# Top-32 attention: the third eight is sunk by GpSimd, the fourth eight found a tile later, and half of the marking done by ScalarE

## The chip, the cores and the metric

The kernel runs on one core of one Trainium2 chip. The metric is the device time of one execution in microseconds (us). TensorE (PE) multiplies, VectorE (DVE), ScalarE (ACT) and GpSimd (POOL) work elementwise, SyncE (SP) issues transfers.

## The reference

Per batch of 8, with 512 queries, 1024 keys and 16 heads of 16 channels: of each row of scores only the 32 largest enter the softmax. An output projection, a gated residual and a mixture of experts follow.

```python
q = (query @ Wq.T + bq).reshape(Bn, Sq, H, DK).transpose(0, 2, 1, 3)
k = (key @ Wk.T + bk).reshape(Bn, -1, H, DK).transpose(0, 2, 1, 3)
scores = jnp.einsum('bhqd,bhkd->bhqk', q, k) / np.sqrt(DK)
vals, idx = jax.lax.top_k(scores, 32)
p = jax.nn.softmax(vals, axis=-1)
ctx = jnp.einsum('bhqk,bhqkd->bhqd', p, gathered_v)
x = x + jnp.tanh(g_xattn[0]) * (ctx @ Wo.T + bo)
x = x + jnp.tanh(g_ffn[0]) * mixture_of_experts(layernorm(x))
```

## The kernel before

The program runs in stages, each a function with one program per engine: project (queries, keys and values, queries and keys cut into three bf16 parts), attend, repair, route, experts, combine. The change lies in attend, with two lines in repair.

attend works on 512 tiles T of 128 queries and one head, four tiles (QT) to a head H, sixteen (TILES) to an iteration I. Every engine's program is written out by hand as a loop over steps s; what it does in a step is for tiles some steps back, and semaphores alone tie the engines together.

- TensorE: `scores` (L415) makes the scores of a tile in ps_s, two steps ahead. `mark` (L429, L436) makes the transposed scores of a whole head for two of its eight key blocks in ps_e (L429, with three rows of the row's maximum to subtract), and adds -2^100 through `big` for each score that `side` marks as under the 32nd (L436). `count` (L446) sums the marks, `turn_peak`, `values` and `turn_out` handle the maxima, the product with the values and the turned result.
- ScalarE: `copy` (L505) brings ps_s to one of four buffers `sc`, once the tile four back has been marked (`sided`); `shift` (L510) takes the maxima; `exp` (L516) takes ps_e to pT; `take_out` (L523) the result; `count_mask` and `sum_counts` once in sixteen tiles.
- VectorE: `chunks` (L564) finds the best eight of each of 24 chunks of a tile. The step is cut into eight slots of three chunks; behind each slot stands one instruction for the tile before: `pick` (first eight), `best_of_rest`, `cull`, `pick` (second eight), `cull`, `round_of` (third eight, L598), `cull` (L591, the third eight taken out of 80 candidates), `round_of` (fourth eight). The last of the fourth eight is the 32nd value. `invert` and `normalise` come once a head.
- GpSimd: `to_sides` (L664) writes 1 into `side` where a score is under the 32nd value, 0 elsewhere; `cut_peaks` cuts a head's maxima into bf16 parts; `find_odd` tells, once in sixteen tiles, whether the chunks may have held back a candidate.

repair sums what count and find_odd have left and makes a list of the tiles whose marks are not exactly 32 a row. It then does each of these again from the start, one after the other (a memset of g_s, L795, on GpSimd opens each).

```python
    FIRST = 7
    SIDES = 12
    END = NT + 12
```

FIRST is by how many steps the first mark of a head trails its first tile.

Of the kernel before, what the change touches and what calls it, by code (L numbers as in the profile page):

```python
# [7 lines left out]
BF16 = mybir.dt.bfloat16  # L8
# [285 lines left out]
def attend(nc, pl, io, scr, keep):  # L294
# [5 lines left out]


    G, TILES, KB, HG, DK, VW, KR, S, S2, QT = pl.G, pl.TILES, pl.KB, pl.HG, pl.DK, pl.VW, pl.KR, pl.S, pl.S2, pl.QT
    CH, NA, NC = pl.CH, pl.NA, pl.NC
    NT, NH = pl.ITER * TILES, pl.ITER * HG
    SHIFT = 3
    PAIRS = KB // 2
    FIRST = 7
    SIDES = 12
    END = NT + 12
    assert pl.TT == pl.ITER and QT == 4 and PAIRS == QT and KB == 8  # L310
    with ExitStack() as ctx:
# [8 lines left out]
        identb = sb("a_identb", [P, P], BF16)  # L320
        big = sb("a_big", [P, P], BF16)
        stack = sb("a_stack", [P, VW])
        sc = sb("a_sc", [P, 4, S2])
# [4 lines left out]
        above = sb("a_above", [P, 2, TILES, 2])  # L328
        rest = sb("a_rest", [P, 2, QT])
        peak = sb("a_peak", [P, 2, QT, SHIFT], BF16)  # L330
# [26 lines left out]
        culled = sem("a_culled")  # L357
        topped = sem("a_topped")
        odd_part = sem("a_odd_part")
# [4 lines left out]
        shifted = sem("a_shifted")  # L364
        sided = sem("a_sided")
        marked = sem("a_marked")
# [37 lines left out]
        def _(pe):  # L404
            pe.wait_ge(consts, 8 + TILES)

# [12 lines left out]
            def mark(H, n):  # L419

                u, j = H // HG % 2, H % HG
                if n == 0:
                    pe.wait_ge(shifted, H + 1)
                if H or n:
                    pe.wait_ge(expd, PAIRS * H + n)
                for i in range(2):
                    k = 2 * n + i
                    keys = slice(k * P, (k + 1) * P)
                    nc.tensor.matmul(ps_e[:, i * S:(i + 1) * S], ks[:, u, j, keys], qs[:, u, j, :], start=True, stop=False)  # L429
                if n == 0:  # L430
                    pe.wait_ge(sided, QT * H + QT)
                for i in range(2):
                    k = 2 * n + i
                    keys = slice(k * P, (k + 1) * P)
                    for qt in range(QT):
                        mm = nc.tensor.matmul(ps_e[:, i * S + qt * P:i * S + (qt + 1) * P],  # L436
                                              side[:, (QT * H + qt) % SIDES, keys], big[:], start=False, stop=qt == QT - 1)
                mm.then_inc(marked, 1)

            def count(T):  # L440
                I, i = T // TILES, T % TILES
                if i == 0 and I:
                    pe.wait_ge(summed, I)
                pe.wait_ge(sided, T + 1)
# [35 lines left out]

            for s in range(-2, END):
                H, n = head_at(s, FIRST)
                if H is not None:
                    mark(H, n)
                if 0 <= s - 4 < NT:
                    count(s - 4)
# [3 lines left out]
                H, n = head_at(s, 5)  # L490
                if H is not None and n == 0:
                    turn_peak(H)
                H, n = head_at(s, 13)
                if H is not None and n == 0:
                    turn_out(H)
                if s + 2 < NT:
                    scores(s + 2)

        @block.scalar
        def _(act):  # L500
            def copy(T):
                act.wait_ge(scored, T + 1)
                if T >= 4:
                    act.wait_ge(sided, T - 3)
                nc.scalar.copy(sc[:, T % 4, :], ps_s[:]).then_inc(copied, 1)  # L505

# [30 lines left out]

            for s in range(-1, END):
                if s + 1 < NT:
                    copy(s + 1)  # L540
                H, n = head_at(s, 6)
                if H is not None and n == 0:
                    shift(H)
                H, n = head_at(s, FIRST)
                if H is not None:
                    exp(H, n)
                H, n = head_at(s, 12)
                if H is not None and n == 0:
                    take_out(H)
                I, i = divmod(s - 4, TILES)  # L550
                if i == TILES - 1 and 0 <= I < pl.ITER:
                    sum_counts(I)
                I, i = divmod(s, TILES)
                if i == 9 and I < pl.ITER:
                    count_mask(I)

        @block.vector
        def _(dve):
            SLOTS = 8

            def chunks(T, n0, n1):
                c = cand[:, T % 4, :]
                for n in range(n0, n1):
                    ins = nc.vector.max(c[:, 8 + n:8 + n + 7 * CH + 1:CH], sc[:, T % 4, pl.cut[n]:pl.cut[n + 1]])  # L564
                if n1 == CH:
                    ins.then_inc(chunked, 1)

            def pick(T, r):
# [4 lines left out]
                else:  # L573
                    dve.wait_ge(culled, 3 * T + 1)
                nc.vector.max(top[:, T // TILES % 2, T % TILES, 8 * r:8 * r + 8], cand[:, T % 4, 8:8 + (r + 1) * CH]
# [6 lines left out]
            def cull(T, r):  # L582

                m = top[:, T // TILES % 2, T % TILES, 8 * r:8 * r + 8]
                if r < 2:
                    dve.wait_ge(picked, 2 * T + r + 1)
                    c = cand[:, T % 4, 8:8 + (r + 1) * CH]
                else:
                    dve.wait_ge(topped, 2 * T + 1)
                    c = cand[:, T % 4, 0:8 + NA]  # L590
                nc.vector.match_replace(c, m, c, TAKEN).then_inc(culled, 1)  # L591

            def round_of(T, r):

                if r == 2:
                    dve.wait_ge(rested, T + 1)
                dve.wait_ge(culled, 3 * T + r)
                nc.vector.max(top[:, T // TILES % 2, T % TILES, 8 * r:8 * r + 8], cand[:, T % 4, 0:8 + NA]).then_inc(topped, 1)  # L598

# [13 lines left out]
            for s in range(END):  # L613
                if s < NT:
                    dve.wait_ge(copied, s + 1)
                H, n = head_at(s, 14)
                for p in range(SLOTS):
# [7 lines left out]
                    if 0 <= T < NT:  # L625
# [6 lines left out]
                        elif p == 3:  # L632
                            pick(T, 1)
                        elif p % 2 == 0:
                            cull(T, p // 2 - 1)
                        else:
                            round_of(T, (p - 1) // 2)

        @block.gpsimd
        def _(pool):  # L640
            nc.gpsimd.memset(ks[KR:KR + SHIFT], -1.0).then_inc(consts, 1)
            pool.wait_ge(consts, 1)
            nc.gpsimd.memset(ident[:], 0.0).then_inc(set0, 1)
            nc.gpsimd.memset(row_of[:], 0.0).then_inc(set0, 1)
# [5 lines left out]
            for c in range(P // VW):  # L650
                nc.gpsimd.affine_select(out=stack[:], in_=stack[:], compare_op=ALU.not_equal, fill=1.0, base=-VW * c,
                                        pattern=[[-1, VW]], channel_multiplier=1).then_inc(consts, 1)
                pool.wait_ge(consts, 3 + c)
            nc.gpsimd.tensor_scalar(big[:], ident[:], -FLOOR, None, ALU.mult).then_inc(consts, 1)
# [4 lines left out]
            def to_sides(T):  # L659

                pool.wait_ge(topped, 2 * T + 2)
                if T >= SIDES:
                    pool.wait_ge(marked, PAIRS * ((T - SIDES) // QT + 1))
                nc.gpsimd.tensor_scalar(side[:, T % SIDES, :], sc[:, T % 4, :],  # L664
                                        top[:, T // TILES % 2, T % TILES, pl.TOPK - 1:pl.TOPK], None, ALU.is_lt
                                        ).then_inc(sided, 1)

# [28 lines left out]

            for s in range(2, NT + 2):
                to_sides(s - 2)
                H, n = head_at(s, 4)
                if H is not None and n == 0:  # L700
                    cut_peaks(H)
                if (s - 2) % TILES == TILES - 1:
                    find_odd((s - 2) // TILES)


def repair(nc, pl, io, scr, keep):
# [7 lines left out]
    with ExitStack() as ctx:  # L714
# [146 lines left out]
        def _(dve):  # L861
# [3 lines left out]
            def link(ins):  # L865
# [7 lines left out]
            dve.wait_ge(in_flat, 16)  # L873
            link(V.tensor_scalar(bad[:].rearrange("p (i n) -> p n i", n=TILES), flat[:], float(P * (S2 - pl.TOPK)), None,
                                 ALU.not_equal))
            link(V.scalar_tensor_tensor(out=bad[:], in0=ps_t[0][0:1, 0:NT], scalar=0.0, in1=bad[:], op0=ALU.is_gt,
# [805 lines left out]
```

## Time and profile before

| | us |
|---|---|
| median of 3 runs (lowest, highest) | 3369.7 (3368.29, 3371.82) |
| the profiled execution | 3371.16 |
| its span, first to last instruction | 3369.4 |
| VectorE busy in the span | 2730.0 |
| TensorE busy | 2526.4 |
| GpSimd busy | 1863.3 |
| ScalarE busy | 1440.1 |
| first to last start of a chunk search | 246.5 to 2168.6 |

The span runs from the first to the last instruction of the profiled execution, and the busy times are inside it. Averages over the span mix stages: attention holds some 1922 us of it, and repair, routing, experts and combination follow. Matmuls are pipelined and their ends modelled, so that a busy TensorE is not one at its peak.

### The profile page before, as it was taken

The page shows a single profiled execution, that of the slowest core. Times are in us where ns is not written, and L with a number is a line of the kernel's source. Part 1 is how long each engine was busy: PE and PEld are TensorE (multiplying, and loading weights), DVE is VectorE, ACT ScalarE, POOL GpSimd, SP SyncE. Part 2 cuts the span into 40 slices and gives each one's busy share as a digit, 9 for nine tenths or more (in the row PEclk, how much of TensorE's full clock was granted, in tenths as well). Part 3 has the DMA queues.
Part 4 walks back from the last instruction along what each step waited for, and adds up shares of the span by engine and source line. Part 5 has one row for each costly group of instructions (what it writes and reads, how often), then busy time and mean ns, then how long its engine had stood idle before and what let it go on. Part 6 is the DMA issues. An engine that isn't in the chain of part 4 may idle for free. (4 is left out here: it accounts for less than half of the span.)

```text
span 3369.4 us, 64915 instructions
## 1 busy us (share of the span) xinstructions
PE 2526.4 (75%) x17711; PEld 1590.3 (47%) x17712; DVE 2730.0 (81%) x20227; ACT 1440.1 (43%) x1942; POOL 1863.3 (55%) x1381
## 2 busy tenths in 40 slices
PE   7827788777778787877787877724705999999990
PEld 5413333333333333333333333313605999999990
DVE  6739999999999999999999999754705666666753
ACT  2215666666666666666666666501101222222220
POOL 1018888888888888888888888600172111111107
PEclk9868999999999999999999999955757999999995
DMA  6870212111121111212112111011222111122106
GB/s 200 249 183 25 53 32 62 32 44 50 32 62 32 47 47 32 62 32 47 47 32 62 32 46 48 1 40 42 76 95 101 65 60 61 49 69 70 67 30 192
DMA packets 141931, 219.60 MB, mean 65 GB/s; under 512 B 22433, under 2 KB 103585, under 8 KB 138497
## 3 DMA queue, kind: packets, MB, share of 16 engines
q1 hardware_dynamic: 116608, 171.43, 18.5%
q0 software_dynamic: 9472, 29.37, 2.8%
q10 hardware_dynamic: 15488, 14.68, 1.3%
q8 instruction: 140, 2.29, 0.3%
q14 instruction: 223, 1.82, 0.2%
HBM read 142.02 MB, written 73.40 MB: 64 GB/s over the span
## 5 line engine op out<-in xcount | busy, mean ns | idle before, releaser
L564 DVE MAX8 a_cand<-a_sc 128x8 f32<-128x43 f32 (+1 forms) x12288 | 1723.7, 215 | 49.8 <-ACT a_sc L505 49.7
L664 POOL TENSOR_SCALAR a_side<-a_sc,a_top 128x1024 bf16<-128x1024 f32 x512 | 1455.0, 2842 | 334.9 <-DVE a_top L598 329.9
L505 ACT COPY a_sc<-a_ps_s 128x1024 f32<-128x1024 f32 x512 | 518.2, 1012 | 780.6 <-POOL a_side L664 720.1
L516 ACT ACTIVATE a_pT<-a_ps_e 128x1024 f32<-128x1024 f32 x512 | 526.5, 1028 | 13.4 <-PE a_ps_e L436 9.7
L415 PE MATMUL a_ps_s<-a_ks,a_qs 96*128 96x512 bf16 x1024 | 320.1, 395 | 246.7 <-ACT a_sc L505 193.6
L429 PE MATMUL a_ps_e<-a_qs,a_ks 99*128 99x512 bf16 x1024 | 316.1, 391 | 179.6 <-ACT a_pT L516 179.0
L468 PE MATMUL a_ps_o<-a_pT,a_vs 128*32 128x512 f32 x2048 | 428.0, 692 | 1.1 <-ACT a_pT L516 1.1
L1351 POOL TENSOR_TENSOR e_wl<-e_raw,e_wh 128x2048 fp32r<-128x2048 f32 x24 | 110.5, 4603 | 521.7 <-DVE e_wh L1488 521.7
L1391 PE MATMUL e_ps_gu<-e_xh,e_wl 128*128 128x256 f32 x1280 | 364.2, 285 | 5.9 <-DVE e_xl L1471 4.0
L1393 PE MATMUL e_ps_gu<-e_xh,e_wh 128*128 128x256 f32 x1280 | 363.4, 284 | 0.0
L1392 PE MATMUL e_ps_gu<-e_xl,e_wh 128*128 128x256 f32 x1280 | 363.4, 284 | 0.0
L436 PEld LDWEIGHTS a_ps_e<-a_big,a_side 128*128 128x128 bf16 x4096 | 284.6, 100 | 128.8 <-issue 12.4
L446 PE MATMUL a_ps_c<-a_side,a_row_of 128*16 128x512 bf16 x1024 | 331.0, 407 | 0.0
L591 DVE MATCH_REPLACE8 a_cand<-a_top,a_cand 128x24 f32<-128x24 f32 (+2 forms) x1536 | 331.0, 215 | 0.0
L436 PE MATMUL a_ps_e<-a_big,a_side 128*128 128x128 bf16 x4096 | 328.9, 225 | 0.0
L415 PEld LDWEIGHTS a_ps_s<-a_ks,a_qs 96*128 96x128 bf16 x1024 | 71.6, 109 | 516.8 <-ACT a_sc L505 341.7
L1503 DVE SCALAR_TENSOR_TENSOR e_sg<-e_th,e_ps_gu 128x256 f32<-128x256 f32 x320 | 134.3, 420 | 192.7 <-ACT e_th L1451 177.3
L1451 ACT ACTIVATE e_th<-e_ps_gu 128x256 f32<-128x256 f32 x320 | 122.6, 383 | 340.0 <-PE e_ps_gu L1393 329.5
L429 PEld LDWEIGHTS a_ps_e<-a_qs,a_ks 99*128 99x128 bf16 x1024 | 76.5, 98 | 379.3 <-issue 211.1
L598 DVE MAX8 a_top<-a_cand 128x8 f32<-128x80 f32 x1024 | 252.2, 246 | 2.0
L1391 PEld LDWEIGHTS e_ps_gu<-e_xh,e_wl 128*128 128x128 f32 x1280 | 247.1, 193 | 7.2 <-DVE e_xl L1471 4.7
L1392 PEld LDWEIGHTS e_ps_gu<-e_xl,e_wh 128*128 128x128 f32 x1280 | 247.2, 193 | 0.0
(206 smaller groups left out, 4120.4 us busy)
## 6 DMA issues: line engine op xcount, KB each, us to landing
scr_v<-p_vp SPq DMA_DIRECT2D x32, 512.0 KB, 5.9
a_vs<-scr_v SPq DMA_DIRECT2D x32, 512.0 KB, 5.8
a_mask<-in_mask SPq DMA_DIRECT2D x32, 512.0 KB, 6.6
scr_k<-p_kp SPq DMA_DIRECT2D x96, 128.0 KB, 2.4
a_ks<-scr_k SPq DMA_DIRECT2D x32, 384.0 KB, 4.5
a_qs<-scr_q SPq DMA_DIRECT2D x192, 64.0 KB, 5.2
scr_disp<-a_zeros SPq DMA_DIRECT2D x32, 320.0 KB, 7.0
e_xin<-scr_disp SPq DMA_DIRECT2D x40, 256.0 KB, 2.7
```

The source lines that it names most:

```text
L415: mm = nc.tensor.matmul(ps_s[:, h * 512:(h + 1) * 512], qs[0:KR, u, j, qt * P:(qt + 1) * P], ks[0:KR, u, j, h * 512:(h + 1) * 512], start= ...
L429: nc.tensor.matmul(ps_e[:, i * S:(i + 1) * S], ks[:, u, j, keys], qs[:, u, j, :], start=True, stop=False)
L436: mm = nc.tensor.matmul(ps_e[:, i * S + qt * P:i * S + (qt + 1) * P], side[:, (QT * H + qt) % SIDES, keys], big[:], start=False, stop=qt = ...
L446: mm = nc.tensor.matmul(ps_c[0:TILES, :], row_of[:, i, :], side[:, T % SIDES, h * 512:(h + 1) * 512], start=(i == 0 and h == 0), stop=(i = ...
L468: mm = nc.tensor.matmul(ps_o[VW * c:VW * (c + 1), :], vs[:, u, k, VW * j:VW * (j + 1)], pT[:, k, :], start=(half == 0), stop=(half == 1), ...
L505: nc.scalar.copy(sc[:, T % 4, :], ps_s[:]).then_inc(copied, 1)
L516: nc.scalar.activation(pT[:, 2 * n:2 * n + 2, :].rearrange("p k q -> p (k q)"), ps_e[:], ACT.Exp).then_inc(expd, 1)
L564: ins = nc.vector.max(c[:, 8 + n:8 + n + 7 * CH + 1:CH], sc[:, T % 4, pl.cut[n]:pl.cut[n + 1]])
L664: nc.gpsimd.tensor_scalar(side[:, T % SIDES, :], sc[:, T % 4, :], top[:, T // TILES % 2, T % TILES, pl.TOPK - 1:pl.TOPK], None, ALU.is_lt) ...
L1391: nc.tensor.matmul(out, al, bh, start=(k == 0), stop=False)
L1392: nc.tensor.matmul(out, ah, bl, start=False, stop=False)
L1393: mm = nc.tensor.matmul(out, ah, bh, start=False, stop=(k == n - 1))
```

## The change

The third cull leaves VectorE. After the third eight, GpSimd does `sink`: it makes `gone`, which is -3e38 wherever a candidate is at or above the 24th value, and adds it to the candidates as `left`. `round_of(T, 3)` takes the fourth eight from `left`, one step later than before. `to_sides` stays on GpSimd for the first two tiles of a head. For the other two GpSimd does `step_under`, two operations on one column that give `next_under`, the next number under the 32nd value, and ScalarE marks by Sign of next_under minus score: -1 for a kept score, 1 for one under it. So `mark` first adds -2^100 to these two tiles through `onesb` and `floor`, then the sides, and the scores last. There are six buffers `sc` for four; marks, counts and what follows them come one step later.

```diff
-    FIRST = 7
+    FIRST = 8
+    SCORES = 6
+    HALF = QT // 2
     SIDES = 12
-    END = NT + 12
+    END = NT + 14
...
+        def sided_by(T):
+
+            by = T % QT // HALF
+            return sided[by], T // QT * HALF + T % HALF + 1
...
+                if n == 0:
+                    for by in sided:
+                        pe.wait_ge(by, HALF * H + HALF)
                 for i in range(2):
                     k = 2 * n + i
                     keys = slice(k * P, (k + 1) * P)
-                    nc.tensor.matmul(ps_e[:, i * S:(i + 1) * S], ks[:, u, j, keys], qs[:, u, j, :], start=True, stop=False)
-                if n == 0:
-                    pe.wait_ge(sided, QT * H + QT)
-                for i in range(2):
-                    k = 2 * n + i
-                    keys = slice(k * P, (k + 1) * P)
+                    nc.tensor.matmul(ps_e[:, i * S + HALF * P:(i + 1) * S], onesb[:], floor[:], start=True, stop=False)
                     for qt in range(QT):
-                        mm = nc.tensor.matmul(ps_e[:, i * S + qt * P:i * S + (qt + 1) * P],
-                                              side[:, (QT * H + qt) % SIDES, keys], big[:], start=False, stop=qt == QT - 1)
+                        nc.tensor.matmul(ps_e[:, i * S + qt * P:i * S + (qt + 1) * P], side[:, (QT * H + qt) % SIDES, keys],
+                                         big[:], start=False, stop=False)
+                    mm = nc.tensor.matmul(ps_e[:, i * S:(i + 1) * S], ks[:, u, j, keys], qs[:, u, j, :],
+                                          start=False, stop=True)
                 mm.then_inc(marked, 1)
...
         @block.scalar
         def _(act):
+            def to_sides(T):
+
+                act.wait_ge(under_set, T // QT * HALF + T % HALF + 1)
+                if T >= SIDES:
+                    act.wait_ge(marked, PAIRS * ((T - SIDES) // QT + 1))
+                nc.scalar.activation(side[:, T % SIDES, :], sc[:, T % SCORES, :], ACT.Sign, bias=next_under[:, T % 8:T % 8 + 1],
+                                     scale=-1.0).then_inc(sided[1], 1)
+
             def copy(T):
                 act.wait_ge(scored, T + 1)
-                if T >= 4:
-                    act.wait_ge(sided, T - 3)
-                nc.scalar.copy(sc[:, T % 4, :], ps_s[:]).then_inc(copied, 1)
+                if T >= SCORES:
+                    act.wait_ge(*sided_by(T - SCORES))
+                nc.scalar.copy(sc[:, T % SCORES, :], ps_s[:]).then_inc(copied, 1)
...
                 if s + 1 < NT:
                     copy(s + 1)
-                H, n = head_at(s, 6)
+                if 0 <= s - 4 < NT and (s - 4) % QT >= HALF:
+                    to_sides(s - 4)
+                H, n = head_at(s, 7)
...
+                else:
+                    dve.wait_ge(sunk, T + 1)
+                    src = left[:, T % 2, :]
+                nc.vector.max(top[:, T // TILES % 2, T % TILES, 8 * r:8 * r + 8], src).then_inc(topped[r - 2], 1)
...
-                        elif p % 2 == 0:
+                        elif p == 2 or p == 4:
                             cull(T, p // 2 - 1)
-                        else:
-                            round_of(T, (p - 1) // 2)
+                        elif p == 5:
+                            round_of(T, 2)
+                    if p == 6 and 0 <= s - 2 < NT:
+                        round_of(s - 2, 3)
...
+            def step_under(T):
+
+                n = T // QT * HALF + T % HALF + 1
+                pool.wait_ge(topped[1], T + 1)
+                last = top[:, T // TILES % 2, T % TILES, pl.TOPK - 1:pl.TOPK]
+                one = slice(T % 8, T % 8 + 1)
+                nc.gpsimd.tensor_scalar(gap[:, one], last, 1.0 + 2.0 ** -23, -2.0 ** -124, ALU.mult, ALU.add
+                                        ).then_inc(gap_set, 1)
+                pool.wait_ge(gap_set, n)
+                nc.gpsimd.tensor_scalar(next_under[:, one], last, 1.0 - 2.0 ** -24, gap[:, one], ALU.mult, ALU.min
+                                        ).then_inc(under_set, 1)
+
+            def sink(T):
+
+                src, g = cand[:, T % 4, 0:8 + NA], gone[:, T % 2, :]
+                pool.wait_ge(topped[0], T + 1)
+                nc.gpsimd.tensor_scalar(g, src, top[:, T // TILES % 2, T % TILES, 23:24], TAKEN, ALU.is_ge, ALU.mult
+                                        ).then_inc(found, 1)
+                pool.wait_ge(found, T + 1)
+                nc.gpsimd.tensor_tensor(left[:, T % 2, :], src, g, ALU.add).then_inc(sunk, 1)
...
-            for s in range(2, NT + 2):
-                to_sides(s - 2)
+            for s in range(2, NT + 3):
+                if s - 2 < NT:
+                    sink(s - 2)
+                T = s - 3
+                if T >= 0 and T % QT < HALF:
+                    to_sides(T)
+                elif T >= 0:
+                    step_under(T)
```

In repair the expected sum of marks is P x (1024 - 32) for the first two tiles of a head, as before for all, and P x (1024 - 64) for the other two.

On VectorE, in the middle of attention, from one tile's second cull to the next tile's first instruction (a_top holds the eights, a_cand the candidates). Before:

```order
L591 MATCH_REPLACE a_cand<-a_top,a_cand 128x48 [waits a_picked]
L564 MAX a_cand<-a_sc 128x8 x3
L598 MAX a_top<-a_cand 128x8 [waits a_culled,a_rested]
L564 MAX a_cand<-a_sc 128x8 x3
L591 MATCH_REPLACE a_cand<-a_top,a_cand 128x80 [waits a_topped]
L564 MAX a_cand<-a_sc 128x8 x3
L598 MAX a_top<-a_cand 128x8 [waits a_culled]
L564 MAX a_cand<-a_sc 128x8 [waits a_copied]
L564 MAX a_cand<-a_sc 128x8 x2
L575 MAX a_top<-a_cand 128x8 [waits a_chunked]
```

Now:

```order
L592 MAX a_cand<-a_sc 128x8 x3
L626 MAX a_top<-a_cand 128x8 [waits a_culled,a_rested]
L592 MAX a_cand<-a_sc 128x8 x3
L626 MAX a_top<-a_left 128x8 [waits a_sunk]
L592 MAX a_cand<-a_sc 128x8 x3
L592 MAX a_cand<-a_sc 128x8 [waits a_copied]
L592 MAX a_cand<-a_sc 128x8 x2
L603 MAX a_top<-a_cand 128x8 [waits a_chunked]
```

The cull over 80 candidates is gone, the round that reads a_left, of the tile before, has its slot, and two slots of three searches follow each other.

On GpSimd, in the second half of a head's cycle, now (before, each tile had one L664 there):

```order
L716 TENSOR_SCALAR a_gone<-a_cand,a_top 128x80 [waits a_topped2]
L719 TENSOR_TENSOR a_left<-a_cand,a_gone 128x80 [waits a_found]
L696 TENSOR_SCALAR a_side<-a_sc,a_top 128x1024 [waits a_marked,a_topped3]
L716 TENSOR_SCALAR a_gone<-a_cand,a_top 128x80 [waits a_topped2]
L719 TENSOR_TENSOR a_left<-a_cand,a_gone 128x80 [waits a_found]
L696 TENSOR_SCALAR a_side<-a_sc,a_top 128x1024 [waits a_marked,a_topped3]
L742 CAST a_peak<-a_top 128x4 [waits a_picked,a_peak_turned]
```

A sink stands before each marking, and the head's cut_peaks (its first row is the last one here) behind the second of two markings.

## Rows read from the trace of the kernel before

**Rows 1.** The page, part 1: busy us (share of the span) x instructions.

```profile
PE 2526.4 (75%) x17711; PEld 1590.3 (47%) x17712; DVE 2730.0 (81%) x20227; ACT 1440.1 (43%) x1942; POOL 1863.3 (55%) x1381
```

**Rows 2.** Busy time by stretch: PE, PEld, DVE, ACT, POOL, PEclk, DMA share, GB/s.

```profile
1200.00:1600.00 400.00, 318.13 (x2246) 143.77 (x2243) 399.60 (x3781) 247.72 (x293) 326.19 (x237) 0.95 0.18 43
...
460.00:520.00 60.00, 49.78 (x339) 22.32 (x339) 60.00 (x570) 37.31 (x45) 49.04 (x36) 0.91 0.15 39
```

**Rows 3.** The page, part 5, VectorE's chunk searches: busy, mean ns, idle before.

```profile
L564 DVE MAX8 a_cand<-a_sc 128x8 f32<-128x43 f32 (+1 forms) x12288 | 1723.7, 215 | 49.8 <-ACT a_sc L505 49.7
```

**Rows 4.** Timeline of VectorE within one step: start us, us, what.

```profile
1201.39 0.44 DVE L564 MAX8 a_cand<-a_sc 128x8 f32<-128x42 f32 x3
...
1203.72 0.44 DVE L564 MAX8 a_cand<-a_sc 128x8 f32<-128x42 f32 x3
1204.03 0.11 DVE L591 MATCH_VALUE_LOAD a_cand<-a_top,a_cand 128x8 f32 x1
...
1204.23 0.45 DVE L564 MAX8 a_cand<-a_sc 128x8 f32<-128x42 f32 x3
...
1204.69 0.44 DVE L564 MAX8 a_cand<-a_sc 128x8 f32<-128x42 f32 x3
...
1205.09 0.44 DVE L564 MAX8 a_cand<-a_sc 128x8 f32<-128x42 f32 x3
```

**Rows 5.** Timeline of the second step, in brackets idle time before.

```profile
249.39 0.40 DVE L564 MAX8 a_cand<-a_sc 128x8 f32<-128x42 f32 x3
...
252.88 2.86 POOL L664 TENSOR_SCALAR a_side<-a_sc,a_top 128x1024 bf16<-128x1024 f32 x1 [15.66 <-DVE a_top L598]
...
253.08 0.41 DVE L564 MAX8 a_cand<-a_sc 128x8 f32<-128x42 f32 x3
```

**Rows 6.** Groups of GpSimd: busy us, mean ns, idle before.

```profile
L664 POOL TENSOR_SCALAR a_side<-a_sc,a_top 128x1024 bf16<-128x1024 f32 x512 | 1455.0, 2842 | 334.9 <-DVE a_top L598 329.9 <-PE a_ps_e L436 4.2 <-issue 0.2
...
L695 POOL TENSOR_TENSOR a_peak<-a_rest,a_peak 128x4 bf16<-128x4 f32 x128 | 26.3, 206 | 10.2
...
L672 POOL TENSOR_TENSOR a_above<-a_top 128x32 f32<-128x32 f32 x32 | 9.4, 295 | 0.0
L675 POOL TENSOR_SCALAR a_above<-a_above 128x32 f32<-128x32 f32 x32 | 9.3, 292 | 3.0
...
L654 POOL TENSOR_SCALAR a_big<-a_ident 128x128 bf16<-128x128 f32 x1 | 0.6, 566 | 0.1
```

**Rows 7.** Groups of ScalarE.

```profile
L516 ACT ACTIVATE a_pT<-a_ps_e 128x1024 f32<-128x1024 f32 x512 | 526.5, 1028 | 13.4 <-PE a_ps_e L436 9.7
L505 ACT COPY a_sc<-a_ps_s 128x1024 f32<-128x1024 f32 x512 | 518.2, 1012 | 780.6 <-POOL a_side L664 720.1 <-PE a_ps_s L415 60.5
...
L853 ACT ACTIVATE g_ex<-g_s,g_nmax 128x1024 f32<-128x1024 f32 x5 | 5.7, 1148 | 69.2 <-DVE g_nmax L910 69.2
```

**Rows 8.** Timeline of TensorE, turns, scores and a mark.

```profile
1208.77 0.39 PE L456 MATMUL a_ps_r<-a_identb,a_peak 128*3 128x128 bf16 x4 [0.20 <-POOL a_peak L695]
...
1210.00 0.60 PE L415 MATMUL a_ps_s<-a_ks,a_qs 96*128 96x512 bf16 x2
1210.43 0.60 PE L429 MATMUL a_ps_e<-a_qs,a_ks 99*128 99x512 bf16 x2
1210.87 0.61 PE L436 MATMUL a_ps_e<-a_big,a_side 128*128 128x128 bf16 x8
1211.41 0.60 PE L446 MATMUL a_ps_c<-a_side,a_row_of 128*16 128x512 bf16 x2
```

**Rows 9.** First and last chunk search (view of line 564), and the stage's end.

```profile
L564 DVE MAX8 a_cand<-a_sc x12288: 183/214/261, 246.5 to 2168.6; 128x8 f32<-128x43 f32 x132, 128x8 f32<-128x42 f32 x67
...
2177.49 1.02 ACT L516 ACTIVATE a_pT<-a_ps_e 128x1024 f32<-128x1024 f32 x1 [1.22 <-PE a_ps_e L436]
...
2189.61 0.62 SPq L802 DMA_DIRECT2D g_flat<-lows  x1
```

**Rows 10.** Timeline of GpSimd in the repair stage.

```profile
2223.37 0.95 POOL L795 MEMSET g_s<- 128x1024 f32 x1 [20.52 <-DVEq L781]
...
2295.97 0.95 POOL L795 MEMSET g_s<- 128x1024 f32 x1 [23.17 <-DVEq L781]
```

More of the change, by code:

```diff
@@ L321, in attend @@
         big = sb("a_big", [P, P], BF16)
+        onesb = sb("a_onesb", [P, P], BF16)
+        floor = sb("a_floor", [P, HALF * P], BF16)
         stack = sb("a_stack", [P, VW])
-        sc = sb("a_sc", [P, 4, S2])
+        sc = sb("a_sc", [P, SCORES, S2])
         side = sb("a_side", [P, SIDES, S2], BF16)
@@ L328, in attend @@
         above = sb("a_above", [P, 2, TILES, 2])
+        gone = sb("a_gone", [P, 2, 8 + NA])
+        left = sb("a_left", [P, 2, 8 + NA])
+        gap = sb("a_gap", [P, 8])
+        next_under = sb("a_next_under", [P, 8])
         rest = sb("a_rest", [P, 2, QT])
@@ L357, in attend @@
         culled = sem("a_culled")
-        topped = sem("a_topped")
+        topped = [sem(f"a_topped{n}") for n in (2, 3)]
+        found = sem("a_found")
+        sunk = sem("a_sunk")
+        gap_set = sem("a_gap_set")
+        under_set = sem("a_under_set")
         odd_part = sem("a_odd_part")
@@ L364, in attend @@
         shifted = sem("a_shifted")
-        sided = sem("a_sided")
+        sided = [sem(f"a_sided_{n}") for n in ("pool", "act")]
         marked = sem("a_marked")
@@ L404, in _ @@
         def _(pe):
-            pe.wait_ge(consts, 8 + TILES)
+            pe.wait_ge(consts, 10 + TILES)
             def scores(T):
@@ L484, in _ @@
                     mark(H, n)
-                if 0 <= s - 4 < NT:
-                    count(s - 4)
+                if 0 <= s - 5 < NT:
+                    count(s - 5)
                 H, n = head_at(s, FIRST + 2)
@@ L489, in _ @@
                     values(H, n // 2)
-                H, n = head_at(s, 5)
+                H, n = head_at(s, 6)
                 if H is not None and n == 0:
                     turn_peak(H)
-                H, n = head_at(s, 13)
+                H, n = head_at(s, 14)
                 if H is not None and n == 0:
@@ L546, in _ @@
                     exp(H, n)
[L547 removed]
+                H, n = head_at(s, 13)
                 if H is not None and n == 0:
                     take_out(H)
[L550 removed]
+                I, i = divmod(s - 5, TILES)
                 if i == TILES - 1 and 0 <= I < pl.ITER:
@@ L642, in _ @@
             pool.wait_ge(consts, 1)
+            nc.gpsimd.memset(onesb[:], 1.0).then_inc(consts, 1)
+            nc.gpsimd.memset(floor[:], -FLOOR / P).then_inc(consts, 1)
             nc.gpsimd.memset(ident[:], 0.0).then_inc(set0, 1)
@@ L701, in _ @@
                     cut_peaks(H)
-                if (s - 2) % TILES == TILES - 1:
-                    find_odd((s - 2) // TILES)
+                if T >= 0 and T % TILES == TILES - 1:
+                    find_odd(T // TILES)
 def repair(nc, pl, io, scr, keep):
@@ L873, in _ @@
             dve.wait_ge(in_flat, 16)
-            link(V.tensor_scalar(bad[:].rearrange("p (i n) -> p n i", n=TILES), flat[:], float(P * (S2 - pl.TOPK)), None,
-                                 ALU.not_equal))
+            of_tile = bad[:].rearrange("p (i j t) -> p j t i", j=HG, t=QT)
+            sums = flat[:].rearrange("p (j t) i -> p j t i", t=QT)
+            half = QT // 2
+            for h, right in ((slice(0, half), P * (S2 - pl.TOPK)), (slice(half, QT), P * (S2 - 2 * pl.TOPK))):
+                ins = V.tensor_scalar(of_tile[:, :, h], sums[:, :, h], float(right), None, ALU.not_equal)
+            link(ins)
             link(V.scalar_tensor_tensor(out=bad[:], in0=ps_t[0][0:1, 0:NT], scalar=0.0, in1=bad[:], op0=ALU.is_gt,
```

28 lines of the change are left out of this document (12 added, 16 removed).

## The prediction

> **What bounds the kernel now.** I read the page first: VectorE is busy for 2730.0 of 3369.4 us, more than any other engine [rows 1]. Then the stretches: in the attention stage VectorE is busy for 399.6 of 400 us, TensorE for 318.1, GpSimd for 326.2 and ScalarE for 247.7 [rows 2]. Then the groups: over 12288 chunk searches VectorE stood 49.8 us before them, 49.7 of it once, before the first [rows 3]. So VectorE sets the pace of attention, and only what leaves its queue can shorten a tile. The last view is its order in time. A tile's step is 24 chunk searches in eight slots of three, with one instruction of the tile before behind each three. Three searches alone take 0.31 us (1203.72 to 1204.03), the slot with the third cull 0.51 (to 1204.23), the slot with a round 0.46 (to 1204.69), a whole step 3.70 (1201.39 to 1205.09) [rows 4]. One step in four also carries a reciprocal and a product, so the mean is 3.75: the searches start from 246.5 to 2168.6 us, 1922 us for 512 tiles [rows 9].
>
> **VectorE.** The third cull goes, two instructions by the row (value load and replace). Slots six and seven took 0.51 + 0.46; they become a slot with the fourth round, 0.46, and a bare slot, 0.31. That is 0.20 us a tile, on the path, and 512 x 0.20 = **102 us**. The new step is 3.55 on the mean, 14.2 us a head of four tiles.
>
> **GpSimd.** It gains two operations over 128x80 a tile (sink) and loses half of its 2.84 us markings. No row has 128x80. The nearest are 0.29 us for 128x32 (L672, L675) and 0.57 for 128x128 (L654) [rows 6]; I take 0.43 each, in the middle of the two, and 0.09 for each start behind a wait, 1.05 a sink, with 0.75 and 1.3 as ends. The two 128x1 steps for a tile that ScalarE marks I take at 0.27 each with their wait, by the 0.21 of the 128x4 rows (L695); cut_peaks has four such, 1.1. A head then costs 4 x 1.05 + 2 x 2.90 + 2 x 0.54 + 1.1 + 0.3 (find_odd, once in four heads) = 12.5 of 14.2 us, and 13.5 at the upper end. It stays hidden. The fourth round of a tile now waits for its sink, with all later VectorE work behind it. Tightest is the head's fourth tile, whose sink stands behind two markings and cut_peaks. From the second tile's sink, ready 2.85 us into a step: 1.05 + 2.90 + 1.05 + 2.90 + 1.1 + 1.05 = 10.05, done at 12.9, against 3 x 3.55 + 3.0 = 13.7 for the round's slot. That leaves 0.8 us, and none at the upper end. I cost it at nothing.
>
> **ScalarE.** Two Signs of 128x1024 a head, with a bias per partition. The row of the same form is the 1.15 us Exp of the repair stage (L853), against 1.03 for Exp without such a bias (L516) [rows 7]. A tile is then 1.01 + 1.03 + 1.15/2 + about 0.4 for the shorter copies and sums = 3.0 of 3.55 us. The Sign waits for next_under, which GpSimd sets early in the third step after the tile's own; behind the Sign stand an Exp and the next copy. That copy is needed more than a step later, since there are six score buffers where there were four. Nothing reaches VectorE.
>
> **TensorE.** Each mark gains two 256-column products with the ones, and the 512-column products move behind the sides. Two products of 512 columns take 0.44 us (1210.43 to 1210.87) [rows 8], so two of 256 take half of that, 0.22 a tile, and a mark goes from 0.98 (1210.43 to 1211.41) to 1.20; weight loads beside a busy array could hold it to the same or stretch it by their own, 0.1 each, to 1.4. At 318.1/400 x 3.75 = 2.98 us of busy time a tile, TensorE comes to 3.2 of 3.55.
>
> **The ends.** Two more fills at the start lie ahead of the loads: 0.3 us. At the end, the last search starts at 2168.6 and the next stage's first transfer at 2189.6, 21 us [rows 9]. The last head now waits for sink, a later round, next_under and two Signs, so that its first Exp (2177.49 now) comes some 2 us later behind the last search, and its marks are 0.22 longer each; 3 us with the start.
>
> **The repair.** A tile whose candidates may be wrong is flagged and done again, one after the other: five memsets of g_s, from 2223.37 to 2295.97 three tiles, 24.2 us each [rows 10]. The change alters who is flagged. Sink takes out everything at or above the 24th value, so that a tie of the 24th and 25th now flags the tile; Sign gives 0 for a score that equals next_under, one last bit under the 32nd, and flags it in two tiles of four. I counted both on the reference's inputs, with scores from the kernel's split into three bf16 parts and last bits disturbed 18 times: the old rule flags 3 to 6 tiles (the trace: 5), the new one 0 to 3 more, one or two in 14 of 18, and one in all three countings that gave 5 before. I take one, **+24 us**, and keep 0 (nothing) and 3 (73) as ends.
>
> **Sum.** The profiled execution took 3371.2 us, a span of 3369.4 and 1.8 around it; 3371.2 - 102 + 3 + 24 = 3296. The runs' median is 1.5 below that execution, so 3295.
>
> **A rule against this change.** VectorE's steps are as long beside GpSimd as without: the step from 249.39 to 253.08 takes 3.69 with GpSimd standing until 252.88 [rows 5], and 3.70 beside its markings [rows 4]. The Trainium skill (Perfetto Trace Analysis, Optimizing Scalar/DVE Operations) warns that the two share a read port, so that handing work from one to the other may not help; by that rule the sum would lose its gain, by the rows it keeps it.
>
> **Rivals.**
> 1. TensorE and ScalarE pace each other: the next mark waits for an Exp, each copy for its scores, and one step of a head has count, values and the turns on TensorE, then scores, copy, Sign and shift before the next Exp. Followed with no overlap across steps, a head's steps take about 3.0, 3.0, 5.5 and 2.4 us (the turns, 1208.77 to 1210.00, are 1.2 of it; a mark and an Exp 2.4) and 0.4 for mask and sums: 14.3 against 14.2. For it: stretches at the lower clock, granted 0.91 in one of 60 us [rows 2], which lengthen the TensorE part of 14.3 to some 14.8. Against it: the next mark can run beside copy and Sign, and six buffers smooth single slow heads. It would give 3295 + 13 to 3295 + 77, so 3308 to 3372. Chance 0.13.
> 2. Slower: GpSimd paces. It decides when a sink costs over 1.7 us, where a head reaches 15.0 us, today's 4 x 3.75. At 0.9 us an operation, which is more than twice what I interpolate, a head is 8.3 + 4 x 2.0 = 16.3, a tile 4.07, and 512 x (4.07 - 3.75) = +164, with ends and repair 3560. For it: two of the three new forms are in no row. Against it: 128x128 took 0.57. Chance 0.06.
> 3. Not what it says: the Sign does not resolve the last bit, and all 256 of its tiles are repaired, 256 x 24.2 = 6195 us more, 9490. For it: no row shows a Sign of such differences. Against it: the sign of a difference of neighbouring values needs no more than an exact subtraction. Chance 0.03. The Trainium skill (ScalarE: Activation LUTs, Step-by-step: what each stage is for) says that scale and bias are one fused step with a single rounding; by that, this does not happen. No run here shows it.
> 4. VectorE stands while GpSimd reads, the rule above as a mechanism: each sink would hold it for 0.86 us, 512 x (0.86 - 0.20) = +338, with ends and repair 3735. Rows 4 and 5 speak against. Chance 0.02.
>
> **How the numbers follow.** VectorE pacing has 0.76: with no further repair 3271 (0.17), one 3295 (0.33), two 3319 (0.18), three or more from 3343 (0.08). The range from 3267 to 3345 holds these but a little, and half of rival 1; outside are rivals 2 to 4 and the rest, 0.2. A measurement here tells 0.2%, 7 us. Faster by more: 0.75 and nearly all of rival 1, 0.86; within it 0.03; slower 0.11.
>
> **What would show it.** Right: a bare slot of 0.31 us and a step of 3.50 on VectorE; no idle time before the round on a_left; GpSimd's 128x80 operations near 0.43; Signs near 1.15 us; six memsets of g_s. Idle time of VectorE before its chunk searches, released by ScalarE's copies, would mean rival 1; before the round on a_left, rival 2. A span off by steps of 24 us with the step as forecast means that the flagged tiles were miscounted.

## The result, and the profile after

The changed kernel takes 3286.8 us in the median (3284.0 to 3290.2), and the kernel before 3369.0 in the same session (3367.5 to 3371.8): a ratio of 0.976, with a 95% interval of 0.974 to 0.977. The forecast was 3295, in a range from 3267 to 3345. The profiled execution took 3286.27 us with a span of 3284.6, so 84.8 of span are to be found.

The page, part 1, of the changed kernel: busy us (share of the span) x instructions, beside [rows 1].

```profile
PE 2541.3 (77%) x18762; PEld 1653.7 (50%) x18763; DVE 2632.4 (80%) x19222; ACT 1713.0 (52%) x2201; POOL 1735.8 (53%) x2664
```

The same stretch of attention as in [rows 2], with the columns of that view:

```profile
1200.00:1600.00 400.00, 337.92 (x2606) 165.80 (x2604) 399.68 (x3781) 321.22 (x366) 317.07 (x532) 0.99 0.19 46
```

VectorE is still busy for 399.7 of 400 us, so it still sets the pace. It passes the stage sooner because its step holds less. The view of its chunk searches (first and last start), as in [rows 9]:

```profile
L592 DVE MAX8 a_cand<-a_sc x12288: 179/195/238, 248.3 to 2060.9; 128x8 f32<-128x43 f32 x132, 128x8 f32<-128x42 f32 x67
```

The searches now take 2060.9 - 248.3 = 1812.6 us, 3.540 a tile; before, 1922.1 and 3.754. Its timeline within one step, to be laid beside [rows 4]:

```profile
1200.35 0.39 DVE L592 MAX8 a_cand<-a_sc 128x8 f32<-128x42 f32 x3
...
1202.53 0.21 DVE L626 MAX8 a_top<-a_cand 128x8 f32<-128x80 f32 x1
1202.68 0.39 DVE L592 MAX8 a_cand<-a_sc 128x8 f32<-128x42 f32 x3
1202.99 0.22 DVE L626 MAX8 a_top<-a_left 128x8 f32<-128x80 f32 x1
1203.13 0.70 DVE L592 MAX8 a_cand<-a_sc 128x8 f32<-128x42 f32 x6
1203.76 0.16 DVE L603 MAX8 a_top<-a_cand 128x8 f32<-128x24 f32 x1
1203.84 0.39 DVE L592 MAX8 a_cand<-a_sc 128x8 f32<-128x42 f32 x3
```

The step is 1200.35 to 1203.84, 3.49 us where it was 3.70. The two slots at issue are the one with the fourth round (1202.68 to 1203.13, 0.45) and the bare one, half of the six searches from 1203.13 to 1203.76 (0.31): 0.76 where they took 0.51 + 0.46.

What the other engines took over, from the groups of instructions (busy, mean ns of one, idle before):

```profile
L531 ACT COPY a_sc<-a_ps_s 128x1024 f32<-128x1024 f32 x512 | 516.8, 1009 | 166.5 <-PE a_ps_s L433 159.2
...
L524 ACT ACTIVATE a_side<-a_sc,a_next_under 128x1024 bf16<-128x1024 f32 x256 | 295.1, 1153 | 162.6 <-POOL a_next_under L709 162.6
...
L716 POOL TENSOR_SCALAR a_gone<-a_cand,a_top 128x80 f32<-128x80 f32 x512 | 293.9, 574 | 260.7 <-DVE a_top L626 260.5
L719 POOL TENSOR_TENSOR a_left<-a_cand,a_gone 128x80 f32<-128x80 f32 x512 | 180.6, 353 | 42.7
...
L626 DVE MAX8 a_top<-a_left 128x8 f32<-128x80 f32 x512 | 117.3, 229 | 3.7 <-POOL a_left L719 3.7
```

The last row of the groups is the one to look at: VectorE waited for GpSimd's sink for 3.7 us in all, and those stand at the end of the stage, once. ScalarE's copies no longer wait for GpSimd's marks (720 us in [rows 7]) but for TensorE's scores, 159 us, none of which reaches VectorE: its searches stood for a copy once, for 47.2 us before the first. From the start of a sink to the start of the marking behind it GpSimd takes 0.98 us:

```profile
1210.16 0.56 POOL L716 TENSOR_SCALAR a_gone<-a_cand,a_top 128x80 f32<-128x80 f32 x1
1210.81 0.35 POOL L719 TENSOR_TENSOR a_left<-a_cand,a_gone 128x80 f32<-128x80 f32 x1
1211.14 2.85 POOL L696 TENSOR_SCALAR a_side<-a_sc,a_top 128x1024 bf16<-128x1024 f32 x1
```

The price lies in the repair stage, in the timeline of GpSimd there, as in [rows 10]:

```profile
2098.17 0.95 POOL L854 MEMSET g_s<- 128x1024 f32 x1 [10.99 <-remote]
2119.51 0.95 POOL L854 MEMSET g_s<- 128x1024 f32 x1 [20.39 <-DVEq L840]
...
2215.25 0.95 POOL L854 MEMSET g_s<- 128x1024 f32 x1 [22.95 <-DVEq L840]
2250.03 0.20 POOL L1103 MEMSET r_ident<- 128x128 f32 x1 [33.83 <-POOLq L773]
```

In the kernel before, the first memset and r_ident's are these:

```profile
2201.89 0.95 POOL L795 MEMSET g_s<- 128x1024 f32 x1 [11.07 <-remote]
...
2331.12 0.20 POOL L1040 MEMSET r_ident<- 128x128 f32 x1 [34.20 <-POOLq L714]
```

There are six memsets where there were five, and from the first to r_ident's, which opens the next stage, it is 151.9 us; before, it was 129.2. The whole account of the span: searches -109.5, their start +1.8, from the last search to the repair stage's first transfer +4.1 (25.1 for 21.0), repair +22.6, all later stages -3.7; the sum is -84.7.

### The profile page after: what moved, and what is told of

The parts are those of the page before. It is cut to its first block and busy times, and to the rows that moved or that the text cites. A ratio compares the mean times of both kernels' runs of the same rounds, so it can differ in the third digit from the quotient of the medians.

```text
span 3284.6 us, 67760 instructions
## 1 busy us (share of the span) xinstructions
PE 2541.3 (77%) x18762; PEld 1653.7 (50%) x18763; DVE 2632.4 (80%) x19222; ACT 1713.0 (52%) x2201; POOL 1735.8 (53%) x2664
## 5 line engine op out<-in xcount | busy, mean ns | idle before, releaser
L592 DVE MAX8 a_cand<-a_sc 128x8 f32<-128x43 f32 (+1 forms) x12288 | 1614.1, 198 | 47.3 <-ACT a_sc L531 47.2
L696 POOL TENSOR_SCALAR a_side<-a_sc,a_top 128x1024 bf16<-128x1024 f32 x256 | 729.3, 2849 | 0.0
L450 PE MATMUL a_ps_e<-a_floor,a_onesb 128*128 128x256 bf16 x1024 | 285.1, 278 | 275.7 <-issue 136.3
L716 POOL TENSOR_SCALAR a_gone<-a_cand,a_top 128x80 f32<-128x80 f32 x512 | 293.9, 574 | 260.7 <-DVE a_top L626 260.5
L452 PE MATMUL a_ps_e<-a_big,a_side 128*128 128x128 bf16 x4096 | 400.9, 221 | 0.0
L454 PE MATMUL a_ps_e<-a_qs,a_ks 99*128 99x512 bf16 x1024 | 397.5, 388 | 0.0
L524 ACT ACTIVATE a_side<-a_sc,a_next_under 128x1024 bf16<-128x1024 f32 x256 | 295.1, 1153 | 162.6 <-POOL a_next_under L709 162.6
L486 PE MATMUL a_ps_o<-a_pT,a_vs 128*32 128x512 f32 x2048 | 372.8, 608 | 1.1 <-ACT a_pT L542 1.1
L452 PEld LDWEIGHTS a_ps_e<-a_big,a_side 128*128 128x128 bf16 x4096 | 318.2, 98 | 93.5 <-issue 2.3
L450 PEld LDWEIGHTS a_ps_e<-a_floor,a_onesb 128*128 128x128 bf16 x1024 | 100.6, 98 | 482.2 <-ACT a_pT L542 252.9
```

Of the source, the lines that this page charges most:

```text
L450: nc.tensor.matmul(ps_e[:, i * S + HALF * P:(i + 1) * S], onesb[:], floor[:], start=True, stop=False)
L454: mm = nc.tensor.matmul(ps_e[:, i * S:(i + 1) * S], ks[:, u, j, keys], qs[:, u, j, :], start=False, stop=True)
L486: mm = nc.tensor.matmul(ps_o[VW * c:VW * (c + 1), :], vs[:, u, k, VW * j:VW * (j + 1)], pT[:, k, :], start=(half == 0), stop=(half == 1), ...
L696: nc.gpsimd.tensor_scalar(side[:, T % SIDES, :], sc[:, T % SCORES, :], top[:, T // TILES % 2, T % TILES, pl.TOPK - 1:pl.TOPK], None, ALU.is_lt
```

## The experiments

Each is the changed kernel with the edit shown, except where the text says that it is the kernel before.

**The marking without the sink.** The third cull goes back to VectorE, and the fourth round to its old slot in the same step; ScalarE still marks two tiles of four, and the buffers and the later marks stay.

```diff
+                if r == 2:
+                    dve.wait_ge(topped[0], T + 1)
+                    c = cand[:, T % 4, 0:8 + NA]
+                    nc.vector.match_replace(c, m, c, TAKEN).then_inc(sunk, 1)
+                    return
...
-                    src = left[:, T % 2, :]
+                    src = cand[:, T % 4, 0:8 + NA]
...
-                if s - 2 < NT:
-                    sink(s - 2)
```

> The change with the third cull back on VectorE and no sink; ScalarE still marks two tiles of four, with six buffers and the later marks. Theory (VectorE's queue alone sets the pace): the step goes back to 3.75 us, 0.21 x 512 = 109 us more than the changed kernel, so about 3390, or 3366 if only the sink's ties flagged the sixth tile (then five memsets of g_s). Rival (the gain comes from relieving GpSimd, or from the buffers): it stays below 3320.

Measured: 3368.9 us, a ratio of 1.000 (0.999 to 1.001). GpSimd's load fell to 204 of 400 us, and nothing came of it:

```profile
1200.00:1600.00 400.00, 336.28 (x2447) 159.34 (x2446) 399.21 (x3775) 303.99 (x346) 204.00 (x289) 0.96 0.18 43
...
L592 DVE MAX8 a_cand<-a_sc x12288: 179/198/282, 246.1 to 2169.3; 128x8 f32<-128x43 f32 x132, 128x8 f32<-128x42 f32 x67
...
L859 POOL MEMSET g_s<- 128x1024 f32 x5 | 4.8, 952 | 100.7 <-DVEq L845 89.7 <-remote 11.1
```

The searches take 1923.2 us, as before the change. And there are five memsets, as before the change: by this count Sign flags no further tile, and the sixth comes with the sink.

**The sink without the marking.** GpSimd sinks, and marks all four tiles; TensorE's marks have the products of before, without the one with the ones, and repair expects the sums of before for all tiles. The cut shows ScalarE's and GpSimd's part.

```diff
-                if 0 <= s - 4 < NT and (s - 4) % QT >= HALF:
-                    to_sides(s - 4)
...
-                if T >= 0 and T % QT < HALF:
+                if T >= 0:
                     to_sides(T)
-                elif T >= 0:
-                    step_under(T)
```

> The sink without ScalarE's marks: GpSimd marks all four tiles, the marks on TensorE are as before, the rest as in the change. By the trace of the change GpSimd then needs 4 x (0.57 + 0.35 + 0.2) + 4 x 2.90 + 1.1 + 0.3 = 17.5 us a head. Theory (GpSimd becomes the bound): 4.38 us a tile, 512 x (4.38 - 3.54) = 430 us over the change, about 3715, and VectorE stands before the round on a_left. Rival (VectorE's queue sets the pace whatever GpSimd does): 3287. Six memsets of g_s if the sink's ties flagged the sixth tile, five if the Sign did.

Measured: 3573.6 us, a ratio of 1.061 (1.059 to 1.063). The direction was right, the size 141 us too high. The timeline of GpSimd in it shows why: a sink and a marking, start to start, take 3.81 us.

```profile
1200.02 0.57 POOL L712 TENSOR_SCALAR a_gone<-a_cand,a_top 128x80 f32<-128x80 f32 x1
1200.67 0.35 POOL L715 TENSOR_TENSOR a_left<-a_cand,a_gone 128x80 f32<-128x80 f32 x1
1201.01 2.85 POOL L692 TENSOR_SCALAR a_side<-a_sc,a_top 128x1024 bf16<-128x1024 f32 x1
1203.83 0.56 POOL L712 TENSOR_SCALAR a_gone<-a_cand,a_top 128x80 f32<-128x80 f32 x1
```

A sink is 0.99 there, starts included, and a marking 2.82; with cut_peaks, about 1 a head, a head takes some 16.2 us. The searches (247.0 to 2341.7) took 4.09 a tile, 16.4 a head. VectorE's wait has moved to the row named in the prediction, and with the sink alone there are six memsets:

```profile
L588 DVE MAX8 a_cand<-a_sc x12288: 183/194/214, 247.0 to 2341.7; 128x8 f32<-128x43 f32 x132, 128x8 f32<-128x42 f32 x67
...
L622 DVE MAX8 a_top<-a_left 128x8 f32<-128x80 f32 x512 | 125.0, 244 | 234.6 <-POOL a_left L715 233.1
...
L848 POOL MEMSET g_s<- 128x1024 f32 x6 | 5.7, 951 | 123.8 <-DVEq L834 112.8 <-remote 11.1
```

So the two halves are worth 0 and +205 us alone, and -82 together: moving the marks makes the room on GpSimd in which the sink is hidden.

**Both kernels without repair.** The count of flagged tiles is taken as 0 in the changed kernel, and in the kernel before.

```diff
-            link(V.tensor_copy(total[:], number[:]))
+            link(V.tensor_scalar(total[:], number[:], 0.0, None, ALU.mult))
```

> The changed kernel with the count of flagged tiles set to 0, so that no tile is repaired. Theory: six tiles fall away, 6 x 24 = 144 us, to about 3143. Rival (the time between the memsets is hidden elsewhere): less than 100 us.

> The kernel before with the count of flagged tiles set to 0. Theory: five tiles fall away, about 121 us, to 3248; against the change without repair the pipeline alone then gains 105 us, more than the 82 us that the two kernels show with repair. Rival: the difference stays 82.

Measured: 3136.5 us for the changed kernel and 3235.9 for the one before. So six tiles cost 150.4 us and five 132.8, some 25 to 27 each, and without repair the change gains 99.4: the repair gives back a sixth of it, 17.6 us by these medians. (Forecast were 24 a tile and a gain of 105; the repair stage itself was 22.6 longer in the trace above.)

**How much room GpSimd has.** One more operation over 128x80 a tile, ahead of the sink's own, with a tile and a semaphore of its own (not in the cut); nothing reads its result.

```diff
+                nc.gpsimd.tensor_scalar(gone_too[:, T % 2, :], src, top[:, T // TILES % 2, T % TILES, 23:24], TAKEN,
+                                        ALU.is_ge, ALU.mult).then_inc(found_too, 1)
```

> The changed kernel with one more 128x80 operation on GpSimd a tile, ahead of the sink, its result unused. By the trace of the change and of the sink alone a head on GpSimd then costs 4 x (0.98 + 0.65) + 2 x 2.82 + 2 x 0.65 + 0.98 + 0.25 = 14.7 us against 14.16 of VectorE. Theory (GpSimd is hidden with little to spare): it paces at 3.68 to 3.9 us a tile, 70 to 185 us over the change, 3360 to 3470, with VectorE standing before the round on a_left. Rival (GpSimd has ample room): 3287, no idle time there.

Measured: 3366.9 us, a ratio of 1.000 (0.999 to 1.001). The searches (244.5 to 2134.3) took 3.691 a tile. The row on a_left answers the one with 3.7 above, and the timeline shows one sink, up to the next marking:

```profile
L594 DVE MAX8 a_cand<-a_sc x12288: 189/207/239, 244.5 to 2134.3; 128x8 f32<-128x43 f32 x132, 128x8 f32<-128x42 f32 x67
...
L628 DVE MAX8 a_top<-a_left 128x8 f32<-128x80 f32 x512 | 123.5, 241 | 68.6 <-POOL a_left L725 68.1
...
L720 POOL TENSOR_SCALAR a_gone_too<-a_cand,a_top 128x80 f32<-128x80 f32 x512 | 293.9, 574 | 66.3 <-DVE a_top L628 51.7
```

```profile
1203.73 0.56 POOL L720 TENSOR_SCALAR a_gone_too<-a_cand,a_top 128x80 f32<-128x80 f32 x1
...
1205.24 2.85 POOL L698 TENSOR_SCALAR a_side<-a_sc,a_top 128x1024 bf16<-128x1024 f32 x1
```

One small operation eats 77 of the 109.5 us that the searches had gained; the 32 that are left go mostly to the sixth tile and the longer end. In the timeline a sink takes 1.51 us for 0.98. The prediction's chain to a head's fourth round had three sinks and 0.8 us to spare; with sinks of 0.98 it has 1.0, with these -0.6. A head took 14.76 us for 14.16, which is 0.60 more. VectorE's wait, 68.1 us, came in 124 pieces, about one a head, as the chain has it. GpSimd's total work is not the whole reason: it stood 51.7 us for VectorE itself, 0.40 a head, so that its own work filled no more than some 14.4 of the 14.76.

**What would bound next.** Six of the 24 searches of a tile are left out (their candidates stay 0), and the repair too.

```diff
-                        chunks(s, CH * p // SLOTS, CH * (p + 1) // SLOTS)
+                        if p not in (5, 6):
+                            chunks(s, CH * p // SLOTS, CH * (p + 1) // SLOTS)
```

> The changed kernel without repair and without six of the 24 chunk searches of a tile (slots six and seven; the candidates of these chunks stay at 0), to see what paces next. If VectorE alone paced, its step would fall by 0.62 us, 317 us off the 3136 of the change without repair, 2820. Theory: TensorE and ScalarE, which wait for each other, stop it at 3.3 to 3.5 us a tile, so 3015 to 3115, and VectorE stands for ScalarE's copies or for the turned result. If GpSimd stops it instead, VectorE stands before a_left.

Measured: 3063.4 us, 73 less than the changed kernel without repair. The searches (246.2 to 1989.0) took 3.404 a tile. Who is waited for has changed; the view of the searches, groups of VectorE, and one row of its waits from 260 to 2000 us (us in total, times, longest):

```profile
L593 DVE MAX8 a_cand<-a_sc x9216: 189/196/214, 246.2 to 1989.0; 128x8 f32<-128x43 f32 x131, 128x8 f32<-128x42 f32 x66
...
L631 DVE RECIPROCAL a_rden<-a_ps_u 128x4 f32<-128x4 f32 x128 | 23.4, 183 | 109.8 <-PE a_ps_u L496 109.8
L593 DVE MAX8 a_cand<-a_sc 128x8 f32<-128x42 f32 x3072 | 605.9, 197 | 54.8 <-ACT a_sc L532 54.6
L627 DVE MAX8 a_top<-a_left 128x8 f32<-128x80 f32 x512 | 115.9, 226 | 6.4 <-POOL a_left L723 5.8
...
DVE a_cand L593 <- ACT a_sc L532: 34.8, 50, 1.4
```

VectorE now waits mostly for TensorE's turned result (109.8) and in 50 places for ScalarE's copies (34.8; the rest of the 54.6 is the wait before the first search). It is TensorE with ScalarE that comes next, not GpSimd.

**TensorE's addition doubled.** The product with the ones is issued twice, with half the value each.

```diff
+                    nc.tensor.matmul(ps_e[:, i * S + HALF * P:(i + 1) * S], onesb[:], floor[:], start=False, stop=False)
...
-            nc.gpsimd.memset(floor[:], -FLOOR / P).then_inc(consts, 1)
+            nc.gpsimd.memset(floor[:], -FLOOR / P / 2).then_inc(consts, 1)
```

> The changed kernel with the 256-column product of the ones issued twice, each with half of the value: 0.22 us more on TensorE a tile, on the way from one Exp to the next. Theory (TensorE is hidden behind VectorE): within 7 us of 3287. Rival (TensorE and ScalarE already share the pace): up to 0.22 x 512 = 113 us more, 3400.

Measured: 3290.1 us, a ratio to the kernel before of 0.977 (0.975 to 0.979), which is that of the change. TensorE was busy for 357.8 of 400 us, and the searches took 3.540 a tile as without it. What the products add is hidden: 19.9 of 400 us over the changed kernel, 0.18 a tile, with no effect on the step. One row surprised:

```profile
L593 DVE MAX8 a_cand<-a_sc x12288: 190/300/332, 246.7 to 2059.2; 128x8 f32<-128x43 f32 x132, 128x8 f32<-128x42 f32 x67
```

A search is recorded with a median of 300 ns where the changed kernel has 195, at the same pace. The duration of one is not what it costs in the queue.

**Versions with fewer chunks.** If VectorE's queue is the price, a search fewer should help until the next bound or the repair stops it.

```diff
-        self.CH = 24
+        self.CH = 23
```

> The changed kernel with 23 chunks a tile (44 or 45 columns each) where it has 24; the result is the same, only more tiles may be flagged. Theory (VectorE's queue sets the step, GpSimd has 0.5 us a tile to spare and TensorE with ScalarE stand at 3.40): one search of 0.104 us leaves each tile, so 3.44 and 512 x 0.104 = 53 us less; a tile with four of its best 24 in one chunk is flagged, and counted on the reference's inputs that is one tile more (25 us): seven memsets, 3287 - 53 + 25 = 3259. Rival (a search's price goes with its columns, which stay 1024 a tile): no gain in the searches, 3287 + 25 = 3312.

And with 22:

> The changed kernel with 22 chunks a tile (46 or 47 columns each). Theory: two searches of 0.104 leave each tile, but TensorE and ScalarE need 3.40, so 3.40 and 72 us less at most; counted on the reference's inputs, six or seven tiles more are flagged (25 us each, 12 or 13 memsets): 3287 - 72 + 163 = 3378, the whole gain lost. Rival (a search's price goes with its columns): 3287 + 163 = 3450.

Measured: 3273.5 us with 23 chunks (3272.3 to 3277.3), a ratio to the kernel before of 0.972 (0.970 to 0.974), and 3378.0 with 22 (1.002 to 1.004). Rows of 23 first, then of 22:

```profile
L592 DVE MAX8 a_cand<-a_sc x11776: 181/194/230, 247.7 to 2021.8; 128x8 f32<-128x45 f32 x105, 128x8 f32<-128x44 f32 x95
...
L854 POOL MEMSET g_s<- 128x1024 f32 x7 | 6.7, 951 | 145.7 <-DVEq L840 134.7 <-remote 11.1
```

```profile
L592 DVE MAX8 a_cand<-a_sc x11264: 183/195/230, 248.0 to 1982.4; 128x8 f32<-128x47 f32 x108, 128x8 f32<-128x46 f32 x90
...
L854 POOL MEMSET g_s<- 128x1024 f32 x13 | 12.4, 951 | 285.6 <-DVEq L840 272.3 <-remote 13.4
```

The first search taken out saved 38.5 us of the stage (1812.6 to 1774.1, 0.075 a tile) and the second 39.7 (0.078): between the two theories, nearer to the one by searches. The searches that are left are longer. In both runs attention opens with searches in one row, up to the first `pick`; rows of 23 first, then of 22:

```profile
247.69 2.76 DVE L592 MAX8 a_cand<-a_sc 128x8 f32<-128x44 f32 x25 [49.28 <-ACT a_sc L531]
250.36 0.16 DVE L603 MAX8 a_top<-a_cand 128x8 f32<-128x23 f32 x1
```

```profile
248.04 2.71 DVE L592 MAX8 a_cand<-a_sc 128x8 f32<-128x46 f32 x24 [49.78 <-ACT a_sc L531]
250.65 0.17 DVE L603 MAX8 a_top<-a_cand 128x8 f32<-128x22 f32 x1
```

That is 0.107 and 0.109 us a search from start to start, where the six in the changed kernel's timeline took 0.63, 0.105 each. So the searches of a tile give up some 0.06; the rest fits the other instructions, which have fewer candidates to go through (a round reads 77 and 74 for 80).

With 23 the saving is more than the one further tile costs; with 22 seven further tiles take back all that the change and both searches gained. The forecast of 3378 for 22 chunks was met, but not by its mechanism alone: TensorE and ScalarE were to stop the step at 3.40, and it went to 3.388 with VectorE still full. So 23 chunks beat both kernels, by 13 us over the changed one (from another session, in which the kernel before was within 1 us). VectorE was busy for 399.9 of 400 us with 22, so the next bound lies no higher than 3.39 there. The 3.404 with six searches out came at a granted clock of 0.97 in the stage, where the run with 22 chunks had 0.99; whether that is the whole difference stays open.

## Why the prediction was right, point by point

- **VectorE's queue is the price.** Forecast 0.20 us a tile and 102 in all; measured 0.214 and 109.5. In the timeline it was 0.21, so the term was right, and low only by its rounding. The run without the sink takes away just this and ends at the time of before.
- **GpSimd is costed at nothing.** It held. The middle of two rows was a poor price for either operation, 0.43 where they measured 0.57 and 0.35. A sink took 0.98 ahead of a marking, forecast 1.05, and that is in part luck: the two operations were 0.07 dearer together than the 0.86 forecast, and the starts between them far cheaper than 0.09 each. The margin was as thin as the chain said: 0.53 us more a sink, and 70% of what the searches gained is gone.
- **ScalarE and TensorE.** Sign took 1.153 us against the 1.15 taken from the repair stage's row. TensorE's busy time a tile was forecast at 3.2 and came to 337.9/400 x 3.54 = 2.99. The granted clock was 0.99 in this stretch for 0.95, which would make 2.86 of the 2.98 before, if all of that time went with the clock; by this estimate the addition shows as some 0.13 and not 0.22. The doubled product, at nearly the same clock, added 0.18. Both engines stayed hidden.
- **The ends.** Forecast 3, measured 1.8 + 4.1. Over the runs of this document the first search starts between 244.5 and 248.3 us, so the 1.8 may be chance; the 4.1 at the end was forecast at some 2.7, too low. The last head's first Exp, forecast 2 us later behind the last search, came 3.4 later (at 2073.18, 12.3 behind it, for 8.9). In the end of the stage, each link of the chain shows its wait:

```profile
2066.34 0.24 DVE L626 MAX8 a_top<-a_left 128x8 f32<-128x80 f32 x1 [3.68 <-POOL a_left L719]
...
2067.04 1.15 ACT L524 ACTIVATE a_side<-a_sc,a_next_under 128x1024 bf16<-128x1024 f32 x1 [1.40 <-POOL a_next_under L709]
...
2073.18 1.02 ACT L542 ACTIVATE a_pT<-a_ps_e 128x1024 f32<-128x1024 f32 x1 [1.40 <-PE a_ps_e L454]
```

- **The repair.** One further tile, 24 us forecast, 22.6 in the trace. The sink brings it: there are five tiles with Sign and no sink, six with the sink and no Sign. That it is a tie of the 24th and 25th value is the prediction's count and follows from what sink does; no run shows the values. One tile was the likeliest of that count, no more: 0 and 3 were its ends, some 24 us a tile.
- **Not in the sum.** The stages after the repair were 3.7 us shorter here. Between the two runs without repair they were 2.6 longer in the changed kernel (from r_ident's memset to the end: 1036.8 and 1034.2), so this is no effect of the change that these runs can tell.
- **Rival 1** (TensorE and ScalarE pace): its 14.3 us a head was too high. With six searches out a head took 13.6, so steps overlap by at least 0.7 us. Its direction was right: it is the next bound.
- **Rival 2** (GpSimd paces): not here, but the sink alone is this rival, with its wait on a_left. It lies nearer than the prediction put it. By GpSimd's total, a sink of 1.7 us was to be the point from which the kernel gets slower; with one of 1.51 the time was already that of before, mostly through the chain.
- **Rival 3** (Sign fails): fell, by the five memsets.
- **Rival 4** (VectorE stands while GpSimd reads): fell. GpSimd has a sink in every step and a marking in two steps of four, and VectorE's step shrank by just what left it. That speaks against the caution of the Trainium skill (Perfetto Trace Analysis, Optimizing Scalar/DVE Operations) that the prediction weighed. Another of its pages is nearer to the rows: SBUF — State Buffer, Who interferes with whom, says that a VectorE instruction with at most one input in SBUF, outside its two-port modes, does not contend with GpSimd. The searches and rounds have one input each, and the trace agrees: 3.49 a step.

## What to carry to other kernels

When one engine's queue is full, a change is worth the start-to-start time that it takes out of that queue; work that is moved costs nothing only where the engine that takes it has been given room first, and here one operation of 0.57 us decided between -82 and about 0. Price the halves of such a change apart: alone they were worth 0 and +205. Where the path depends on the data (flagged tiles at 25 us each), count how the change alters that on the inputs; it was a sixth of the gain here, and all of it with 22 chunks.

## What the runs showed of the hardware that was not expected

- The recorded duration of a chunk search was 195 ns in one kernel and 300 in another (medians), with both at 3.540 us a tile. The Trainium skill (Perfetto Trace Analysis, DVE / Act Engine Instruction) says that the recorded window lasts until the write is acknowledged, while the next instruction may begin to fetch earlier; that fits rows in which three searches together are recorded at 0.39 us and the next instruction begins 0.31 after they began. Why the one kernel's are longer is open. It need not be the code: the kernel before has a median of 214 ns with its repair and 190 without, with the same attention and 3.754 us a tile in both. Without repair:

```profile
L564 DVE MAX8 a_cand<-a_sc x12288: 179/190/222, 246.1 to 2168.2; 128x8 f32<-128x43 f32 x132, 128x8 f32<-128x42 f32 x67
```

- The granted clock of TensorE in the same stretch of attention was 0.95 before, 0.99 after, 1.00 with the doubled product and 0.86 with the sink alone. In that order TensorE was busy for 318, 338, 358 and 313 of 400 us. Busy time alone does not order them: with the third operation on GpSimd it was busy for 335 at 0.95. (These are means over a stretch, as shares of full speed, and so lie between its two levels, 1.2 and 2.4 GHz.)
- On GpSimd, over 128x80 f32, an operation with a comparison by a column's value and a product took 574 ns, and an addition of two such tiles 353.
